# Mixing stage: one product of 1024 columns per unit over records with two rows stored twice, and the norm factor prepared by GpSimd

## What is computed

```python
bc = jnp.einsum('bti,oi->bto', value, W_bc).reshape(Bsz, Tlen, H, 4, N)
bc = bc / (jnp.sqrt(jnp.sum(bc * bc, axis=-1, keepdims=True)) + EPS)
Bz, Bx, Cz, Cx = (bc[..., 0, :], bc[..., 1, :], bc[..., 2, :], bc[..., 3, :])
...
z = S[..., None] * (z - dtE * A[None, :, :, None] * s + dtE * (Bz_t[..., None] * u_t[:, :, None, :]))
s = s + dtE * z + dtE * (Bx_t[..., None] * u_t[:, :, None, :])
y = jnp.einsum('bhn,bhnd->bhd', Cz_t, z) + jnp.einsum('bhn,bhnd->bhd', Cx_t, s)
...
y = (y + skip * value) * jax.nn.silu(gate)
return jnp.einsum('bti,oi->bto', y, W_out)
```

## Time and profile before

| | |
|---|---|
| time, median of 3 runs | 1438.91 us (1437.36 to 1440.94) |
| profiled execution: own time, span | 1436.9 us, 1435.2 us |
| busy, of the span | PE 1270.1, DVE 978.9, POOL 636.9, ACT 634.1 us |
| PE weight loads (PEld, beside the matmuls) | 701.1 us |
| granted clock of PE, mean | 0.954 of full speed |
| the mixing stage | first products at 267.5 us, last evacuate at 736.5 us |

### The profile page before, as it was taken

The page is one execution under the profiler, slowest core; times in us unless marked ns, Lnnn a source line. Parts: engine busy times, 40 slices in busy tenths (PEclk is TensorE's granted clock), DMA queues, the critical chain, the costliest instruction groups (busy, mean ns, idle before and its releaser), DMA issues. The chain is left out here.

```text
span 1435.2 us, 22220 instructions
## 1 busy us (share of the span) xinstructions
PE 1270.1 (88%) x7528; PEld 701.1 (49%) x7528; DVE 978.9 (68%) x1969; ACT 634.1 (44%) x1519; POOL 636.9 (44%) x815
## 2 busy tenths in 40 slices
PE   4968620899999999999979999899999999989999
PEld 3432200456655555565544545455555555554545
DVE  5898997899998999999931020688778787730100
ACT  3454320345555445455532231566566566722221
POOL 2746461377777787787730000244444344420000
PEclk9988865899999999999989999999999999999999
DMA  2236557434444444333320000200000000000000
GB/s 62 118 161 264 234 231 285 156 131 130 129 130 129 129 130 129 129 129 130 124 96 0 0 0 1 84 1 1 1 1 1 1 1 1 1 0 0 11 4 15
DMA packets 61599, 117.78 MB, mean 82 GB/s; under 512 B 6192, under 2 KB 37552, under 8 KB 59056
## 3 DMA queue, kind: packets, MB, share of 16 engines
q1 hardware_dynamic: 59184, 107.97, 21.7%
q10 hardware_dynamic: 2304, 8.39, 1.4%
HBM read 73.09 MB, written 43.25 MB: 81 GB/s over the span
## 5 line engine op out<-in xcount | busy, mean ns | idle before, releaser
L652 PE MATMUL banks<-w_bc,valueT 128*128 128x512 f32 x512 | 245.6, 604 | 73.3 <-PEq L67 57.7
L1693 POOL TENSOR_SCALAR pr<-pr,rs,sg 128x512 f32<-128x512 f32 (+3 forms) x256 | 151.8, 608 | 207.9 <-DVE rs L1595 207.9
L887 DVE TENSOR_TENSOR pp<-banks,rec 128x512 f32<-128x512 f32 x256 | 164.3, 683 | 6.4 <-DVE banks L873 0.4
L652 PEld LDWEIGHTS banks<-w_bc,valueT 128*128 128x128 f32 x512 | 88.4, 192 | 144.6 <-issue 123.1
L519 POOL TENSOR_TENSOR C<-abL,A 128x1024 f32<-128x1024 f32 x16 | 104.6, 6553 | 92.5 <-DVE X L275 73.0
L1506 ACT ACTIVATE pr<-banks,nm 128x512 f32<-128x512 f32 (+3 forms) x256 | 132.6, 523 | 25.6 <-DVE nm L1589 22.8
L271 DVE TENSOR_TENSOR t<-C,X 128x256 f32<-128x256 f32 x256 | 111.9, 477 | 15.4 <-POOL C L519 15.4
L976 POOL TENSOR_SCALAR_AFFINE_SELECT bp<-bp 128x1024 f32<-128x1024 f32 x64 | 75.2, 1175 | 106.2 <-ACT bp L779 106.2
L1589 DVE TENSOR_REDUCE nm<-banks 128x2 f32<-128x1024 f32 (+3 forms) x128 | 105.5, 824 | 4.4
L1230 DVE TENSOR_TENSOR x<-x,banks 128x256 f32<-128x256 f32 x16 | 6.7, 421 | 148.3 <-PE banks L1141 148.3
L760 ACT ACTIVATE sq<-banks 128x1024 f32<-128x1024 f32 x64 | 65.7, 1026 | 87.2 <-PE banks L652 86.9
(11 more groups left out here) (230 smaller groups left out, 2363.3 us busy)
## 6 DMA issues: line engine op xcount, KB each, us to landing
psi<-X SPq DMA_DIRECT2D x16, 2048.0 KB, 6.4
rec<-psi SPq DMA_DIRECT2D x64, 512.0 KB, 3.8
rec<-psi SPq DMA_DIRECT2D x64, 256.0 KB, 4.0
det<-w_bc ACTq DMA_DIRECT2D x16, 512.0 KB, 4.4
dd<-det SPq DMA_DIRECT2D x64, 128.0 KB, 4.0
w_bc<-in_w_bc SPq DMA_DIRECT2D x1, 4096.0 KB, 15.7
w_bc<-in_f_h SPq DMA_DIRECT2D x4, 1024.0 KB, 7.8
w_bc<-in_f_w SPq DMA_DIRECT2D x6, 256.0 KB, 3.0
```

The source lines that it names most:

```text
L652: mm = pe.matmul(k.bank[q % 4][:], m["valueT"][:, c, t * P:(t + 1) * P], wv[c][:, f, j], start=(c == 0), stop=(c == 1))
L887: ins_ = dve.tensor_tensor(pp[:, q % 2, 4 * ab:4 * ab + 4].rearrange("p (b c) n -> p b c n", b=2), sc[:, 2 * ab:2 * ab + 2].unsqueeze(2).b ...
L1693: pool.tensor_scalar(row, row, rs[:, n // 2 % 2, n % 2, h:h + 1], sg[:, TPB * b + it, hd:hd + 1], ALU.mult, ALU.mult).then_inc(s["scaled"], 1)
```

## The change

1. **Records of 8 rows.** `rec` grows from 6 to 8 rows per unit: rows 2 and 3 of the old record, which both products read, stand twice, so that one instruction reads four pairs of rows that lie one behind the other. SP loads both halves as four rows each: 2 KB a token and unit from `span`, a shifted view of `psi`, and 2 KB from `psi`. Before it were 2 KB and 1 KB.
2. **One product.** `products` is one instruction of 1024 columns instead of two of 512.
3. **The norm factor.** The first step of `scale` leaves DVE. POOL gets `norm(g)`: add eps into `fr`, wait for it (`guard`), multiply with W. `scale(g)` waits for it, takes the reciprocal and multiplies the banks as before. POOL runs norm(p+2) at the head of iteration p, before combine(2p+3). `root` now waits for norm(g-2) instead of DVE's first step of scale(g-2).
4. **Memory.** The small tiles of the moments and `junk` lie in the first rows of `m["u"]`, which are free by then (one more wait on `uz` in `moments`).

```diff
--- before.py
+++ after.py
@@ -566,12 +566,13 @@
         w_bc = m["w_bc"]
         w_out = sb("w_out", P, 2, D)
         skip = sb("skip", P, 2)
-        rec = sb("rec", P, RL, 2, 6, HN)
+        rec = sb("rec", P, RL, 2, 8, HN)
         dd = sb("dd", P, RL, 2, HN)
         sq = sb("sq", P, 2, 4 * HN)
         ss = sb("ss", P, 2, 2, 4 * G4)
         nr = sb("nr", P, 2, 2, 4 * G4)
-        rn = sb("rn", P, 2, 2, 4 * G4)
+        rn = sb("rn", P, 2, 4 * G4)
+        fr = sb("fr", P, 2, 2, 4 * G4)
         pp = sb("pp", P, 2, 8, HN)
         ct = sb("ct", P, RC, G4, 2 * N)
         bp = sb("bp", P, RB, 3, 2, G4, 2 * N)
@@ -587,15 +588,15 @@
         ygc = sb("ygc", P, 2, 2 * N + P)
         oc = sb("oc", P, D)
         yg = sb("yg", P, 2, 2, P)
-        nmean = sb("mx_nmean", P, EARLY)
-        var = sb("mx_var", P, EARLY)
-        std = sb("mx_std", P, EARLY)
-        rstd = sb("mx_rstd", P, EARLY)
+        nmean = m["u"][:, 0, 128:128 + EARLY]
+        var = m["u"][:, 0, 144:144 + EARLY]
+        std = m["u"][:, 0, 160:160 + EARLY]
+        rstd = m["u"][:, 0, 176:176 + EARLY]
         eps = sb("mx_eps", P, 1)
-        junk = sb("mx_junk", P, D)
+        junk = m["u"][:, 0, 0:D]
         rows = m["gateT"][:, 0].rearrange("p (t d) -> p t d", d=D)
         s = {n: sem("mx_" + n) for n in (
-            "eps", "mean", "var", "std", "rstd", "row",
+            "guard", "norm", "eps", "mean", "var", "std", "rstd", "row",
             "o_loaded", "bc", "sq", "ss", "root", "rn", "scaled", "prod", "bt", "ca", "ct", "tp", "qk", "s",
             "pm", "masked", "uz", "hz_clear", "yg", "gs", "tk", "hT", "turned", "hz", "yv", "yg_done", "out", "oc", "x", "ygc",
             "ent_ready", "ent", "pick", "winv")}
@@ -618,6 +619,8 @@
             return 2 * linked.index(t) + f
 
         psi = scratch["psi"].rearrange("(g c) t f -> c t g f", g=HG)
+        span = scratch["psi"].rearrange("(g c) t f -> c g (t f)", g=HG)[:, :, 2 * HN:2 * HN + P * REC].rearrange(
+            "c g (t f) -> c t g f", f=REC)
         det = scratch["det"].rearrange("c t (g f) -> c t g f", g=HG)
 
         @block.sync
@@ -632,9 +635,8 @@
                 if n >= RL:
                     sp.wait_ge(s["prod"], 2 * (n - RL) + 2)
                     sp.wait_ge(s["ct"], 2 * (n - RL) + 2)
-                sp.dma_start(rec[:, r, :, 2:6].rearrange("p g c n -> p g (c n)"), psi[t, 1:P + 1, g]).then_inc(loaded[r], 16)
-                sp.dma_start(rec[:, r, :, 0:2].rearrange("p g c n -> p g (c n)"), psi[t, 0:P, g, 2 * HN:4 * HN]
-                             ).then_inc(loaded[r], 16)
+                sp.dma_start(rec[:, r, :, 0:4].rearrange("p g c n -> p g (c n)"), span[t, :, g]).then_inc(loaded[r], 16)
+                sp.dma_start(rec[:, r, :, 4:8].rearrange("p g c n -> p g (c n)"), psi[t, 1:P + 1, g]).then_inc(loaded[r], 16)
                 sp.dma_start(dd[:, r], det[t, :, g]).then_inc(loaded[r], 16)
             sp.wait_ge(s["bc"], UNITS)
             load_ffn(sp, m, weights, k.ffn_loaded[0])
@@ -762,7 +764,7 @@
             def root(g):
                 act.wait_ge(s["ss"], g + 1)
                 if g >= 2:
-                    act.wait_ge(s["rn"], 2 * (g - 2) + 1)
+                    act.wait_ge(s["norm"], g - 1)
                 act.activation(nr[:, g % 2], ss[:, g % 2], ACT.Sqrt).then_inc(s["root"], 1)
 
             def copy_qk(q):
@@ -801,6 +803,7 @@
 
             def moments(t):
                 act.wait_ge(s["x"], t + 1)
+                act.wait_ge(s["uz"], 3)
                 act.activation(junk[:], k.x[:, t], ACT.Copy, scale=-1.0 / D, accum_out=nmean[:, t:t + 1]).then_inc(s["mean"], 1)
                 act.wait_ge(s["mean"], t + 1)
                 act.activation(junk[:], k.x[:, t], ACT.Square, bias=nmean[:, t:t + 1],
@@ -862,15 +865,14 @@
                 t, f, j = split(2 * g)
                 hg = 4 * f + j
                 b = g % 2
-                dve.wait_ge(s["root"], g + 1)
-                dve.scalar_tensor_tensor(out=rn[:, 0], in0=nr[:, b], scalar=NORM_EPS, in1=m["W"][:, t, hg:hg + 2],
-                                         op0=ALU.add, op1=ALU.mult).then_inc(s["rn"], 1)
-                dve.wait_ge(s["rn"], 2 * g + 1)
-                dve.reciprocal(rn[:, 1], rn[:, 0]).then_inc(s["rn"], 1)
+                dve.wait_ge(s["norm"], g + 1)
+                if g >= 1:
+                    dve.wait_ge(s["scaled"], g)
+                dve.reciprocal(rn[:], fr[:, b]).then_inc(s["rn"], 1)
                 dve.wait_ge(s["bc"], 2 * g + 2)
-                dve.wait_ge(s["rn"], 2 * g + 2)
+                dve.wait_ge(s["rn"], g + 1)
                 bank = k.banks[:, 2 * b:2 * b + 2].rearrange("p u (a n) -> p (u a) n", n=N)
-                dve.tensor_tensor(bank, bank, rn[:, 1].rearrange("p u a -> p (u a)").unsqueeze(2).broadcast_to([P, 32, N]),
+                dve.tensor_tensor(bank, bank, rn[:].rearrange("p u a -> p (u a)").unsqueeze(2).broadcast_to([P, 32, N]),
                                   ALU.mult).then_inc(s["scaled"], 1)
 
             def products(q):
@@ -882,12 +884,9 @@
                     dve.wait_ge(s["bt"], q - 1)
                     dve.wait_ge(s["ca"], q - 1)
                 sc = k.bank[q % 4][:].rearrange("p (a n) -> p a n", n=HN)
-                for ab in range(2):
-                    w = rec[:, n % RL, q % 2, 2 * ab:2 * ab + 4].rearrange("p (b c) n -> p b c n", b=2)
-                    ins_ = dve.tensor_tensor(pp[:, q % 2, 4 * ab:4 * ab + 4].rearrange("p (b c) n -> p b c n", b=2),
-                                             sc[:, 2 * ab:2 * ab + 2].unsqueeze(2).broadcast_to([P, 2, 2, HN]), w, ALU.mult)
-                    if ab == 1:
-                        ins_.then_inc(s["prod"], 1)
+                dve.tensor_tensor(pp[:, q % 2].rearrange("p (a c) n -> p a c n", c=2),
+                                  sc.unsqueeze(2).broadcast_to([P, 4, 2, HN]),
+                                  rec[:, n % RL, q % 2].rearrange("p (a c) n -> p a c n", c=2), ALU.mult).then_inc(s["prod"], 1)
 
             def state(t, f):
                 n = links(t, f)
@@ -994,6 +993,16 @@
                 pool.tensor_tensor(cv, cv, dd[:, q // 2 % RL, q % 2].rearrange("p (i n) -> p i n", n=N).unsqueeze(1)
                                    .broadcast_to([P, 2, G4, N]), ALU.mult).then_inc(s["ct"], 1)
 
+            def norm(g):
+                t, f, j = split(2 * g)
+                hg = 4 * f + j
+                pool.wait_ge(s["root"], g + 1)
+                if g >= 2:
+                    pool.wait_ge(s["rn"], g - 1)
+                pool.tensor_scalar(fr[:, g % 2], nr[:, g % 2], NORM_EPS, None, ALU.add).then_inc(s["guard"], 1)
+                pool.wait_ge(s["guard"], g + 1)
+                pool.tensor_tensor(fr[:, g % 2], fr[:, g % 2], m["W"][:, t, hg:hg + 2], ALU.mult).then_inc(s["norm"], 1)
+
             for f in range(2):
                 lanes = k.ident[:].rearrange("p (f j t) -> p f t j", f=2, j=4)[:, f]
                 pool.tensor_copy(pick[:, f].rearrange("p t (j d) -> p t j d", j=4),
@@ -1002,8 +1011,11 @@
             pool.wait_ge(s["uz"], 1)
             expand_u(0)
             expand_u(1)
+            norm(0)
             combine(0)
             for p in range(-1, PAIRS):
+                if p + 2 < PAIRS:
+                    norm(p + 2)
                 if p + 1 < PAIRS:
                     combine(2 * p + 3)
                 if p >= 0:
```

## The result

The changed kernel takes 1546.38 us (1545.73 to 1547.31, 4 runs) against 1438.39 us: ratio 1.0748, 95% interval 1.073 to 1.0767. That is 108 us or 7.5% slower.

What follows compares the result with a forecast made beforehand. PE and DVE were both taken as full in mixing, at 14.35 us per two pairs. Some 30 units x (17.8 - 14.35) = +103 us gave 1541 us for the median, range 1478 to 1575.

Steps and rivals of the forecast that it cites:

- The chain that it named: Loop from scores(p-1) to scores(p+1) through PE, ACT, POOL, DVE and PE: 18.4 us instead of 14.33.
- The place on POOL: norm(p+2) stands behind mask(p-1) and combine(2p+2): reached at 343.21, done 343.86, so `state` at 348.06, 2.5 us later.
- The stall that was to be 3 to 4 us: Sign of being right: PE waits for L887 before L652 some 3 to 4 us every second pair.
- The collision: DVE's `state` and `evacuate` meet busy POOL on shared ports: 3.05 us instead of 1.45.
- The product: DVE's single product of 1024 columns takes 1.25 us to the next start, a gain of some 0.1 per unit.
- The unit: Two pairs, since `state` comes every second pair: 14.35 us before, 17.8 forecast on average, some 30 units.
- The 2 us that the prediction added for each unit with steps of the next layer norm: Three units hold L930 steps; their stall, about 2 us each, adds 0.2 per unit, giving 17.8.
- The clock: Rival that PE's clock falls too: a tenth of the stage at half clock, +29 us, 1570 us; chance 0.04.
- the 1.7 us stall: In the trace before the change, PE waits 1.72 us for L887 and starts at 534.27; PE's busy share there 0.81.
- the likeliest case's own range: 1518 to 1568 us: norm -5 or +8, the products' bounds -2 or +7, the state's time -/+16.
- The likeliest case: Mixing loop with DVE's state steps colliding with POOL: +103 us, 1541 us; chance 0.57.

Runs made afterwards that it cites:

- the four places of `norm`: `norm` moved in POOL's loop of the changed kernel: ahead of the mask 1433.40 us, behind the mask 1454.20, unmoved 1546.38, behind combine(2p+3) 1608.76.
- the added wait: Changed kernel, but POOL waits before combine(2p+4) in state pairs until DVE has finished `state` and `evacuate`: 1506.49 us.
- the part alone: Changed kernel with the norm factor back on DVE; records of 8 rows and the single product stay: 1432.67 us, ratio 0.9965 to the kernel before.
- the reordered kernels: Changed kernel with norm(p+3) behind mask(p), 1454.20 us, or ahead of it, 1433.40 us; the latter with three `pp` buffers, 1430.83 us.
- cutting the first alone: Three buffers of `pp` and three pairs of records, on the changed kernel with norm(p+3) ahead of mask(p): 1430.83 us.
- cutting the second alone: `state` and `evacuate` behind the second products, two buffers of `pp`, on the changed kernel with norm(p+3) ahead of mask(p): 1445.98 us.
- with both cut: Three buffers of `pp`, and `state` and `evacuate` behind the second products, on the changed kernel with norm(p+3) ahead of mask(p): 1423.81 us.
- The kernel with three buffers and the same order: Changed kernel with three buffers of `pp` and three pairs of records, its order untouched: 1546.23 us.

## Why the prediction was right

It said 1541 us and 1546.38 was measured. The chain that it named is the one that the trace shows, step by step; that its number came so near is in part luck, as the last points tell.

- **The place on POOL.** Forecast from the scores: `norm` at 343.21 - 337.70 = 5.51, banks' product 6.66, `products` 7.98, `reduce` 9.23, `state` 10.36. Measured 5.52, 6.64, 7.97, 9.11, 10.23. That this order is the cause is shown by the four places of `norm`, not only by the rows. The stall that was to be 3 to 4 us came as two of PE's waits, 0.72 and 2.52 us.
- **The collision.** 3.05 forecast for `state` and `evacuate`, 2.84 measured; shown as a cause by the added wait. It came about otherwise than forecast: all six steps were to end behind one of POOL's, but in the unit shown only three did so, L901 and the two of L908 beside `combine`, while L896, L917 and L920 kept about their own lengths. In the kernel before, too, such blocks did not always run free: 7 of the 23 before 711 us took 2.4 to 2.8 us.
- **The product.** 1.25 to the next start forecast, 1.14 measured (378.04 to 379.18); the part alone makes the kernel 0.35% faster.
- **The unit.** 18.4 and 17.95 forecast for the carried pairs with a state; 11.27 + 6.77 = 18.04 and, with pairs of 11.00, 17.8 measured. In a tile that isn't carried 17.5 was forecast, with 10.45 + 6.78 = 17.2 measured. In the last tile of a sequence 16.1 and 16.65 were forecast; there 9.41 + 6.34 = 15.8 was measured, since the pairs between are shorter too. The 2 us that the prediction added for each unit with steps of the next layer norm didn't come: two of these units last 8.62 + 8.87 = 17.5, no more than others.
- **The clock, where it was wrong.** "In the stretch with the 1.7 us stall ... the clock stayed at 1.00; so I leave it out." The long stalls of the new kernel are 2.2 to 2.7 us, once in most units outside the last tiles of a sequence, mostly with a shorter one of 0.72 before them, and after 11 of them PE went to the lower of its two levels (1.2 instead of 2.4 GHz). PE's timeline and a stretch:

```profile
322.50 1.98 PE L654 MATMUL banks<-w_bc,valueT 128*128 128x512 f32 x4 [0.72 <-DVE pp L887]
...
327.56 3.78 PE L654 MATMUL banks<-w_bc,valueT 128*128 128x512 f32 x4 [2.48 <-DVE pp L887]
...
331.35 1.06 PE L724 MATMUL banks<-w_out,yg 128*128 128x128 f32 x4
```

```profile
326.00:334.00 8.00, 6.44 (x37) 3.60 (x41) 4.19 (x6) 1.50 (x4) 2.86 (x6) 0.57 0.35 122
```

  Four matmuls take 3.78 instead of 1.98. These 11 state pairs lasted 12.2 to 14.2 us, 1.6 to 3.0 longer than others of their kind; the differences add up to 21 us.
- **Two errors that cancel.** The units at full clock came out some 0.5 us shorter than my 17.8 (17.3 on average over four tiles), about 16 us over 30 units, and the clock, which I had priced at 29 us and put at 4 in 100, gave 21. The likeliest case named the right loop; that its sum was nearer than its terms is luck.
- **A slip in the range.** The terms of the likeliest case's own range, 8, 7 and 16 us above 1541, add up to 1572, not to 1568; the forecast doesn't hang on it.

What the prediction didn't look for were the loops next to the longest one. The expectations for the reordered kernels took TensorE as the bound once the factor was early, and were 9 to 32 us too low. The way through the buffer of `pp` and the way project - square - reduce - state - products are about as long: cutting the first alone changed little (1430.83), cutting the second alone made it worse (1445.98), and only with both cut did the time, 1423.81, come near the 1420 forecast.

## What to carry to other kernels

When work moves to an engine with time to spare, its place in that engine's program can matter more than its length: walk the loop once round, through every instruction that stands ahead of it there and through what these wait for, and compare it with the pace, in each kind of pair and not in one alone. Follow the freed engine as well, since it arrives at other times at buffers and at instructions that it can't run beside. If several loops are of nearly one length, cutting one shows little, and a version has to be tried with all of them cut.

## What was not expected of the hardware

- PE's clock fell after some stalls of 2.5 us and not after others: of the state pairs with a 2.5 us wait at about 366 and 327 us the first kept 1.00 and the second fell to 0.57 over 8 us. Both had the same 0.72 us wait before. The kernel with three buffers and the same order kept 1.00 from 326 to 334 us, in the pair in which the changed kernel fell to 0.57. What decides stays open.
- RECIPROCAL of 32 columns, SBUF to SBUF, took 336 to 356 ns in all its 54 places from 285 to 770 us of the changed kernel, most of them beside a busy GpSimd, and the products with one input in PSUM and one in SBUF 1210 to 1226. Most of what was stretched has two SBUF inputs: L908 has a median of 634 ns there and of 222 in the kernel where GpSimd waits. But not all: of L929, a TENSOR_SCALAR of 128x128 with one SBUF tile as input and two columns as scalars, one took 1173 ns where the mask began beside it, against a median of 346.
